# The steps between two images of a fused attention and edge kernel: from VectorE to ScalarE and GpSimd, and one merge slot moved

## The reference, cut to what matters

```python
x = x + attention(group_norm(x))   # windows of 8x8 tokens, 6 heads; scores from an 8x8 Fourier product
x = x + conv1x1(y + laplacian(y), merge_w) + merge_b,   y = group_norm(x)
```

## Time and profile before

| | |
|---|---|
| three runs, median | 5898.05 us (5894.93 to 5898.69) |
| the profiled execution's own time | 5900.44 us |
| its span, first to last instruction | 5898.6 us |
| mean granted clock of TensorE, of full speed | 0.987 |
| MB read from and written to HBM | 335.82, 201.33 |

### The profile page before, as it was taken

One profiled execution on the slowest core, in us unless ns is written; L12 is line 12 of the kernel. 1 busy time (PEld: TensorE's weight loads), 2 busy tenths in 40 slices (PEclk: granted clock), 3 DMA queues, 4 the chain that ended last, 5 costly groups with the idle time before them and its releaser, 6 DMA issues.

```text
span 5898.6 us, 207339 instructions
## 1 busy us (share of the span) xinstructions
PE 5629.3 (95%) x91644; PEld 4715.9 (80%) x91644; DVE 4388.0 (74%) x7534; ACT 3320.2 (56%) x6404; POOL 3326.2 (56%) x2342
## 2 busy tenths in 40 slices
PE   7999999999999999999999999999999999999977
PEld 5888788888888888887788878888888888888854
DVE  5777777787777777777777778777787787776754
ACT  3666655555555555555555655555555555555522
POOL 1333346665666655665566655665656666666643
PEclk9999999999999999999999999999999999999988
DMA  4222133323333233332333333333333322232245
GB/s 133 74 59 59 56 80 107 106 75 101 98 105 106 78 99 102 107 102 73 101 107 109 91 87 95 103 109 86 91 98 108 107 77 77 82 85 78 80 107 135
DMA packets 392497, 550.51 MB, mean 93 GB/s; under 512 B 24822, under 2 KB 284601, under 8 KB 391610
## 3 DMA queue, kind: packets, MB, share of 16 engines
q1 hardware_dynamic: 391612, 537.24, 32.3%
HBM read 335.82 MB, written 201.33 MB: 91 GB/s over the span
## 4 chain that ended last, share of the span: by engine, by line
PE 80%; ACT 9%; DVE 9%; issue 2%; POOL 0%; SPq 0%; DMA 0%; DVEq 0%; POOLq 0%; ACTq 0%
PE b_q L540 22%; PE b_t L638 7%; PE b_s L656 7%; PE b_q L624 7%; PE b_t L614 6%; PE b_s L488 4%; PE b_t L596 3%; PE b_s L490 3%; PE b_s L547 3%; PE b_s L550 3%; PE b_s L501 3%; ACT qkh L983 2%; PE b_s L499 2%; ACT probs L1056 2%; PE b_s L559 2%; ACT probsT L983 2%
## 5 line engine op out<-in xcount | busy, mean ns | idle before, releaser
L1133 POOL TENSOR_TENSOR probs<-probs,srec 128x768 f32<-128x768 f32 x512 | 881.7, 1722 | 1678.8 <-DVE srec L966 1678.8
L1120 POOL TENSOR_TENSOR probs<-probs,smax 128x768 f32<-128x768 f32 x512 | 755.0, 1475 | 603.9 <-DVE smax L926 603.4
L983 ACT ACTIVATE vs<-b_q 128x192 f32<-128x192 f32 x1024 | 339.7, 332 | 1282.2 <-PE b_q L540 1282.2
L915 DVE TENSOR_TENSOR qkl<-b_q,qkh 128x384 fp32r<-128x384 f32 x1024 | 570.2, 557 | 588.4 <-ACT qkh L983 556.3
L921 DVE TENSOR_TENSOR probs<-b_s,posb 128x768 f32<-128x768 f32 x512 | 490.3, 958 | 676.4 <-PE b_s L656 675.1
L540 PE MATMUL b_q<-wnh,xh 128*128 128x288 f32 x2048 | 703.6, 344 | 68.3 <-DVE qkl L915 65.6
L540 PE MATMUL b_q<-wnl,xh 128*128 128x288 f32 x2048 | 606.8, 296 | 0.0
L540 PE MATMUL b_q<-wnl,xhl 128*128 128x288 f32 x2048 | 605.8, 296 | 0.0
L540 PE MATMUL b_q<-wnh,xl 128*128 128x288 f32 x2048 | 605.7, 296 | 0.0
L540 PE MATMUL b_q<-wnh,xhb 128*128 128x288 f32 x2048 | 605.0, 295 | 0.0
L1095 POOL TENSOR_TENSOR dg<-late 128x645 f32<-128x645 f32 x352 | 563.0, 1599 | 64.3 <-DMA late<-x_dram 50.5
(11 more groups left out here) (159 smaller groups left out, 13871.1 us busy)
## 6 DMA issues: line engine op xcount, KB each, us to landing
ld<-in_x SPq DMA_DIRECT2D x192, 512.0 KB, 4.6
late<-x_dram SPq DMA_DIRECT2D x112, 640.0 KB, 5.1
xs<-in_x SPq DMA_DIRECT2D x128, 512.0 KB, 5.5
x_dram<-late SPq DMA_DIRECT2D x128, 512.0 KB, 2.9
out<-late SPq DMA_DIRECT2D x128, 512.0 KB, 2.9
late<-x_dram SPq DMA_DIRECT2D x240, 192.0 KB, 5.8
xs<-in_x SPq DMA_DIRECT2D x128, 256.0 KB, 5.7
x_dram<-late SPq DMA_DIRECT2D x128, 256.0 KB, 3.6
```

The source lines that it names most:

```text
L915: V.tensor_tensor(qkl[:, i % 2, :], q_out, qkh[:, i % 2, :].bitcast(F32), ALU.subtract).then_inc(lo_out, 1)
L983: return A.activation(o, i, ACT.Copy)
L1120: P.tensor_tensor(probs[:, i % 2, :, :], probs[:, i % 2, :, :], smax[:, i % 2, :].unsqueeze(2).broadcast_to([128, 12, N]), ALU.subtract).t ...
L1133: P.tensor_tensor(probs[:, i % 2, :, :], probs[:, i % 2, :, :], srec[:, i % 2, :].unsqueeze(2).broadcast_to([128, 12, N]), ALU.mult).then_ ...
```

## The change

- Pieces take slots 0, 1, 2, 4, 5, 6, in this order. The small products take slots 3 and 7: `mean` in slot 7 of c = 1, `dev` and `mbias` in c = 2, `gmean` and `gspread` in c = 12, the two `bias` in c = 14. Behind ALONE the task in slot 4 waits for the reader of slot 2, its bank being the same.
- ScalarE reads all small products but `mbias`. It also takes the Sqrts (now in the middle of a double, `weights`), the scaled weights (c = 13, `ph` 4 and 6), the negative mean, the high parts (c = 14), the merge weights (c = 2, `ph` 6) and the borders (`ph` 0, one block later than before).
- GpSimd takes the squared deviations, the Newton steps (of c = 13 behind the stencil in `ph` 2; of c = 2 behind the multiply in `ph` 4) and the remainders of the weights (c = 14 and 15).
- VectorE keeps the aggregations, one per double, the four statistics of the last strip two by two, two reciprocals of 2 columns, and the remainder of the bias rows. TensorE waits for the weights at the head of an image.
- The preparation of the first image stays on VectorE.

```diff
-PIECES = 6
+PIECE_SLOTS = (0, 1, 2, 4, 5, 6)
+LAST_SLOT = PIECE_SLOTS[-1]
...
         def m_task(it):
 
             blk, ph = divmod(it, 8)
-            if ph < PIECES:
+            if ph in PIECE_SLOTS:
                 v = blk - MERGE_LAG
-                return ("piece", v, ph) if 0 <= v < STRIPS else None
+                return ("piece", v, PIECE_SLOTS.index(ph)) if 0 <= v < STRIPS else None
             img, at_blk = divmod(blk, NS)
-            if at_blk == 1 and 1 <= img <= B:
-                return (("mean", "dev")[ph - 6], img - 1, 0)
-            if at_blk == 2 and ph == 6 and 1 <= img <= B:
-                return ("mbias", img - 1, 0)
+            if at_blk == 1 and ph == 7 and 1 <= img <= B:
+                return ("mean", img - 1, 0)
+            if at_blk == 2 and 1 <= img <= B:
+                return (("dev", "mbias")[ph // 4], img - 1, 0)
             if at_blk == 12 and 0 <= img < B - 1:
-                return (("gmean", "gspread")[ph - 6], img + 1, 0)
+                return (("gmean", "gspread")[ph // 4], img + 1, 0)
             if at_blk == 14 and 0 <= img < B - 1:
-                return ("bias", img + 1, ph - 6)
+                return ("bias", img + 1, ph // 4)
             return None
+        def act_reads(it):
+            task = m_task(it)
+            if task and task[0] == "piece":
+                return it >= ALONE and task[2] < 4
+            return task is not None and task[0] != "mbias"
 
...
         m_count, d_count, a_count = {-5: 4}, {-5: 4}, {-5: 0}
         for it in iterations:
-            by_act = it >= ALONE and it % 8 < 4
             m_count[it] = m_count[it - 1] + (m_task(it) is not None)
-            d_count[it] = d_count[it - 1] + (m_task(it) is not None and not by_act)
-            a_count[it] = a_count[it - 1] + (m_task(it) is not None and by_act)
+            d_count[it] = d_count[it - 1] + (m_task(it) is not None and not act_reads(it))
+            a_count[it] = a_count[it - 1] + act_reads(it)
...
-                    m_wait(sp, 8 * (v - 3 + MERGE_LAG) + PIECES - 1)
+                    m_wait(sp, 8 * (v - 3 + MERGE_LAG) + LAST_SLOT)
...
-                m_wait(pe, it - 2 if it > ALONE else it - 1)
+                m_wait(pe, it - 2 if it > ALONE and it % 4 in (1, 2) else it - 1)
                 if pair(2):
                     pe.wait_ge(s_out, pair(2)[1])
                 if kind == "piece":
                     piece(at, p, it)
                 elif kind == "mean":
-                    pe.wait_ge(g2_mean, at + 1)
+                    pe.wait_ge(g2_mean, 2 * (at + 1))
...
+                        pe.wait_ge(lo_w, 2 * img)
+                        pe.wait_ge(bias_w, 2 * img)
...
-                    pe.wait_ge(m_read, d_count[2 * j + 1])
+                    m_wait(pe, 2 * j + 1)
...
-                elif kind == "mean":
...
-                    variance(sm[:, 5, :], sm[:, 4, :])
-                elif kind == "mbias":
+                else:
                     V.tensor_tensor(mc[:, at % 2, :], mb[:, :], m_out[:, 0:2], ALU.subtract).then_inc(m_read, 1)
...
-                else:
...
-                    if u % NS == NS - 1:
+                    if u % NS == NS - 1 and ph in (0, 2):
                         if ph == 0:
                             dve.wait_ge(x1_done, (u + 1) * SD)
-                            for part in range(4):
-                                x1_stats(u, part)
...
-                            last.then_inc(g2_mean, 1)
-                            dve.wait_ge(g2_mean, u // NS + 1)
-                    elif ph % 2 == 0:
+                        for part in (ph, ph + 1):
...
+                    elif u % NS == NS - 1 and ph in (4, 6):
+                        t, m = ((0, CA), (1, CB))[ph // 2 - 2]
+                        dve.wait_ge(g2_stats, 4 * (u // NS + 1))
+                        V.bn_aggr(sm[0:m, 0:2, t], bn1[0:m, t, :, :].rearrange("p k n -> p (k n)")).then_inc(g2_mean, 1)
+                    elif u % NS < NS - 1 and ph % 2 == 0:
                         if ph == 0:
                             dve.wait_ge(x1_done, (u + 1) * SD)
                         x1_stats(u, ph // 2)
...
                 img, c = divmod(blk, NS)
...
-                if blk >= 0 and img + 1 < B and c == 13:
-                    if ph == 1:
-                        group_root()
...
-                if c == 2 and 1 <= img <= B:
...
-                    if ph == 1:
...
+                if blk >= 0 and img + 1 < B and c == 13 and ph == 2:
+                    dve.wait_ge(g1_sd, img + 1)
+                    V.reciprocal(cst[:, 4, :], cst[:, 3, :]).then_inc(g1_rec, 1)
+                if blk >= 0 and img + 1 < B and (c, ph) in ((14, 4), (15, 0)):
...
+                if c == 2 and 1 <= img <= B and ph == 5:
+                    dve.wait_ge(g2_sd, img)
+                    V.reciprocal(sm[:, 7, :], sm[:, 6, :]).then_inc(g2_rec, 1)
...
+                if not act_reads(it):
+                    return
+                kind, v, p = m_task(it)
+                if kind == "piece" and p == 0:
+                    act.wait_ge(out_sent[v % 2], 48 * (v // 2))
...
+                act.wait_ge(m_mm, m_count[it])
+                if kind == "piece":
                     A.activation(res_a[:, v % 2, p * 256:(p + 1) * 256], m_region(it)[:, 0:256], ACT.Identity,
                                  bias=mc[:, v // NS % 2, 0:1]).then_inc(a_read, 1)
...
+                elif kind == "gspread":
+                    copy(cst[:, 0:2, :], m_out[:, 0:4].rearrange("p (t f) -> p f t", t=2)).then_inc(a_read, 1)
+                elif kind == "bias":
...
+                    copy(wnh[first, v % 2, 1, lo:up], m_out[first, 0:QKV // 2])
+                    copy(biashi[second, :], m_out[second, 0:QKV // 2])
+                    copy(biasrow[second, :], m_out[second, 0:QKV // 2]).then_inc(a_read, 1)
+                elif kind == "mean":
+                    copy(sm[:, 2:4, :], m_out[:, 0:4].rearrange("p (t f) -> p f t", t=2)).then_inc(a_read, 1)
+                else:
+                    A.activation(sm[:, 5, 0:1], m_out[:, 0:1], ACT.Identity, bias=sm[:, 7, 0:1])
+                    A.activation(sm[:, 5, 1:2], m_out[:, 2:3], ACT.Identity, bias=sm[:, 7, 1:2]).then_inc(a_read, 1)
+            def border(v):
+                s = v % NS
+                if 3 <= s < NS - 1:
+                    return
+                act.wait_ge(a_read, a_count[8 * (NS * (v // NS + 1) + 1) + 7])
+                if v >= 3:
+                    act.wait_ge(m_mm, m_count[8 * (v - 3 + MERGE_LAG) + LAST_SLOT])
+                if s < 3:
...
+                if s in (0, NS - 1):
...
+                last.then_inc(border_w, 1)
+            def weights(blk, ph):
+                img, c = divmod(blk, NS)
+                b = img + 1
+                if blk >= 0 and b < B:
+                    if (c, ph) == (13, 0):
+                        act.wait_ge(a_read, a_count[8 * (blk - 1) + 7])
+                        A.activation(cst[:, 3, :], cst[:, 1, :], ACT.Sqrt).then_inc(g1_sd, 1)
+                    elif c == 13 and ph > 2:
...
+                        act.wait_ge(g1_root, b)
...
+                        A.activation(wn[:, t, :], wq[:, t, :], ACT.Copy, scale=cst[:, 4, t:t + 1]).then_inc(wn_done, 1)
+                    elif (c, ph) == (14, 0):
...
+                        last.then_inc(norm0_w, 1)
+                    elif c == 14:
...
+                        part, o, t = ((slice(0, 128), wnh, 0), (slice(0, CB), wnh, 1), (slice(CB, 128), wnl, 1))[ph // 2 - 1]
+                        copy(o[part, b % 2, t, :], wn[part, t, :]).then_inc(hi_w, 1)
+                if c == 2 and 1 <= img <= B:
+                    par = (img - 1) % 2
+                    if ph == 4:
+                        act.wait_ge(a_read, a_count[8 * blk + 3])
+                        A.activation(sm[:, 6, :], sm[:, 5, :], ACT.Sqrt).then_inc(g2_sd, 1)
+                    elif ph == 6:
+                        act.wait_ge(g2_root, img)
+                        A.activation(mn[:, par, 0:2, :], wm[:, 0:2, :], ACT.Copy, scale=sm[:, 7, 0:1])
+                        A.activation(mn[:, par, 2:5, :], wm[:, 2:5, :], ACT.Copy, scale=sm[:, 7, 1:2]).then_inc(norm1_w, 1)
...
             for j, pair in doubles():
                 blk, ph = divmod(2 * j, 8)
-                img, c = divmod(blk, NS)
...
                 h = (j + 2) // 2
                 a_result(2 * j)
                 if pair(0):
                     v_copy(2 * j)
                     high(2 * j)
                 split(h, 0 if j % 2 == 0 else 2)
+                weights(blk, ph)
+                if ph == 0 and 0 <= blk - STENCIL_LAG < STRIPS:
+                    border(blk - STENCIL_LAG)
...
+            def link(ins):
+                chain[0] += 1
+                ins.then_inc(pool_chain, 1)
+                pool.wait_ge(pool_chain, chain[0])
+            def newton(var, r, t):
+                link(P.tensor_tensor(t, var, r, ALU.mult))
+                link(P.tensor_tensor(t, t, r, ALU.mult))
```

(40 more changed lines are left out.)

106 lines of the change are left out of this document (46 added, 60 removed).

## The result

The changed kernel takes **5843.7 us** (median of four runs, 5837.3 to 5848.3) against 5898.4 of the kernel before on the same chip (5894.9 to 5902.4): ratio **0.9909**, 95% interval 0.9895 to 0.9923. It is faster, but by 55 us and not by the 147 that were forecast, and outside the range. The profiled execution took 5841.05, its span 5839.3.

What follows compares the result with a forecast made beforehand. TensorE, busy 95% of the span, was taken as the bound, so its waits and own work counted. From 5900.4: -48 - 94 - 9 - 8 + 12 = -147, 5753; less 2.4 for the runs' median, 5751 us, range 5730 to 5797.

Steps and rivals of the forecast that it cites:

- The statistics and borders do not leave the path: Rival, chance 0.03: the excess has causes other than VectorE's small steps, only the slots pay, 5845 us.
- the 94 us of the steps: Saving forecast at main-stage changes of image when VectorE's small steps leave the path: excess 144 us falls to 50.
- Slots: Steady blocks: one odd piece place becomes even, saving 0.44 us a block, 48 us over 109 blocks.
- Excess at the changes: Main-stage time above steady blocks at changes of image: 144 us to fall to 50, saving 94.
- The two first changes: Earliest first and second norm, in blocks without merge pieces: 9 us saved of the 15.3 a later pair saves.
- Tail: Last blocks: 8 us saved in block 129, 12 lost (0 to 20) from block 130 on through bank waits.
- the wait of p 3: Tail from block 130: p 3 waits until ScalarE has read p 2, 0.7 us in each of 17 blocks, 12 lost.
- Table loads: Sqrt's 1.28 us loads delay Exp's path by 0.7 or 0.35; rival, double cost: 5789 us, chance 0.03.
- GpSimd's small operations: GpSimd's chains at the norms: 0.3 us per operation with its link, 0.2 us a change on the path, range 0 to 3.
- VectorE's steps: At changes of image, c = 1 to 4, 12 and 13: all delay from VectorE's small steps goes when they leave.

Runs made afterwards that it cites:

- experiment 1: Changed kernel with one wait added, so SyncE issues the source load some 18 us into a block, not 13: 5750.8 us, ratio 0.9752.
- experiment 2: Kernel before, its source load waiting for the piece of slot 2 in place of slot 3, so issued some 13 us into the block: 5971.5 us.
- 3: Changed kernel, source load held for the piece in slot 4 (one double later): 5825.3 us; or only for slot 1 (one double earlier): 5761.2 us.
- 4: Changed kernel, source load in two parts, 128 channels at the early place, the rest behind the gate of experiment 1: 5753.6 us.
- experiment 5: Kernel before with the change's slots for pieces and small products, all small steps on VectorE, source load at its old time: 5902.1 us, ratio 1.0006.
- experiment 10: Kernel of experiment 1, tail banks given by piece number so p 3 no longer waits for ScalarE's read of p 2, TensorE's waits fitted: 5758.0 us.
- experiment 6: Kernel of experiment 1 with the borders back on VectorE, in the first double of a block: 5752.8 us, ratio 0.9752.
- 8: Kernel of experiment 1, first norm's two scalings and three roundings back on VectorE: apart 5748.2 us; that version with them put together 5749.5 us.
- 9: Kernel of experiment 1 with the statistics of an image's last strip together in the first double of c = 1, on VectorE: 5766.3 us.
- experiment 7: Kernel of experiment 1 with GpSimd's chains of small operations (deviations, root refinements) back on VectorE: 5775.5 us, ratio 0.9792.

## Why the prediction was wrong, and where it was right

**What failed is one sentence**, on the slots: "SyncE's loads and stores of a strip stand behind slots 1 and 3 of the next block, so nothing is later". Nothing is later, but something is earlier: slot 3 is empty after the change, so the source load, and with it the load for the statistics, is let go by slot 2, 5 us sooner. The prediction looked only for lateness. That costs 93 us (experiment 1), it follows the load in the kernel before (experiment 2, 74 us), into double 2 and away again (3), and vanishes with a shorter burst (4). That the data burst as such holds up TensorE's instruction packets is read from the trace (the queues above, the wait for issue, the packet ahead of each of the 29 ends of a wait) and fits all five runs; the runs varied the loads, not the packets. None of the rivals was this one. "The statistics and borders do not leave the path" came nearest in time, 5845 against 5843.7, by luck: it leaves the 94 us of the steps on the path, and experiment 1 has them gone.

**The sum itself** against experiment 1, point by point. That this run ends on the 5751 of the forecast is in part luck, as an oversized term and a term of the wrong sign cancel:

- *Slots*, 42.0 a block with doubles of 10.7, 10.0, 11.0, 10.3: measured 42.04 with 10.69, 9.99, 11.01, 10.36. Right. Yet the term is not one that the slots bring by themselves (experiment 5).
- *Excess at the changes*, 144 to 50, and slots, together -142: the main stage falls from 4763.6 to 4620.6, **-143**. By place: c = 1 0.85 above steady (forecast 0.85), c = 2 1.9 to 2.3 (2.15), c = 3 and 4 nothing; c = 13 0.7 (0.7), c = 14 3.7 (3.6), c = 12 0.15 (0.35).
- *The two first changes*, -9: from the first double to the start of block 19, 759.4 before and 755.4 in experiment 1, **-4**. Oversized; and this stretch goes from 752 to 760 among the other versions of the changed kernel, so the 4 is not clear of that.
- *Tail*, -8 + 12: 283.6 before, 275.9 in the changed kernel, 280.9 in experiment 1, so **-3 to -8** and not +4. (Experiment 2, the kernel before but for the load's place, has 279.8: that place alone moves the stretch by 4 us.) The wait of p 3 came as forecast (0.66 in 16 blocks), but it was no price: the block's length goes with the clock, and without the wait the tail is longer (experiment 10).
- *Table loads*: the Sqrt's of 1.28 stands where forecast, and both neighbours follow at once:

```profile
1526.76 0.62 ACT L949 ACTIVATE xhl<-xs 64x512 fp32r<-64x512 f32 x1
1527.39 1.28 ACT L1040 ACT_TABLE_LOAD   x1
1528.69 0.20 ACT L1040 ACTIVATE sm<-sm 128x2 f32<-128x2 f32 x1
...
1529.13 1.28 ACT L1091 ACT_TABLE_LOAD   x1
1530.42 0.84 ACT L1091 ACTIVATE probs<-probs 128x768 f32<-128x768 f32 x1
```

The Trainium skill, page "ScalarE: Activation LUTs" (What ACT_TABLE_LOAD costs), has about 2.66 us for a switch, a drain included. Here the first load starts when the operation ahead of it ends (1527.38), and the operation behind each load starts 1.30 and 1.29 after the load's start; the drain is not seen.
- *GpSimd's small operations*, 0.3 with the link: 0.19 to 0.28 on average in the changed kernel, with idle time of 0.5 to 0.6 us in all over the 7 or 8 of a line, 0.08 each. Right.
- *VectorE's steps*. The size of what leaves was right, the reason given for it, that all their delay goes with the steps, was too coarse. Borders and wide weights cost nothing on VectorE in the right place (6, 8), the last strip's statistics together 15.5 us (9), the chains 25 (7), nearly all of it one root in an odd place. These are 40 us of the 151 between experiments 5 and 1. The other 110 were not isolated. Block by block, the main stage of experiment 5 is longer than that of experiment 1 by 53 us in c = 13, 30 in c = 1, 26 in c = 12, 22 in c = 2 and 6 in c = 3 and 4. Its kernel has both roots, the three roundings and the negative mean in odd places, and in c = 12 the squared deviation, which the kernel before has in an even one; that these make the rest is argued, not shown.

## What to carry to other kernels

When instructions move, look at everything that counts them. A wait on a shared count is let go by whatever came last before it, so to empty a slot makes a transfer **earlier**, and an earlier transfer can cost as much as a late one. Look also at what stands in the same queue behind what moved. Before moving a small step to another engine, try a place in the order where its own engine waits and its neighbour at the SBUF ports is idle. And a short wait in a stage whose clock comes and goes is not a price until it has been taken away.

## What was not expected of the hardware

- TensorE can run out of instructions, as far as the trace tells. With a burst that holds all 16 DMA engines for some 6 us (1.5 MB) and ends in a stretch where TensorE starts 128 products and as many weight loads in 3.3 us, it waited for issue up to 2.7 us in double 1 (3.5 at one place before the main stage); with 1.0 MB, up to 1.2 us. The same burst some 5 us later cost nothing, and 4 us earlier some 10 us in place of 93. The instruction queue moved 12.04 MB in 735 packets over the run, 16 KB each.
- VectorE operations of two columns took 0.15 or up to 1.5 us, ending within 0.01 us of GpSimd's (experiment 7); the borders' 80 instructions took 39 or 17 us by place (experiment 6).
- In the tail, taking away 0.66 us of waiting in a block lowered the granted clock from 0.90 to 0.76 and made it 10 us longer (experiment 10).
